# Selective scan in pieces of 447 nodes instead of 625, with the sum over the states moved from GpSimd to TensorE

## What is computed

```python
dA = jnp.exp(dt[:, :, None] * A)
dBx = (dt * xc)[:, :, None] * Bm[:, None, :]
def step(h, t):
    dA_t, dBx_t, C_t = t
    h = dA_t * h + dBx_t
    return (h, h @ C_t)
_, y = lax.scan(step, jnp.zeros((xc.shape[1], D_STATE), xs.dtype), (dA, dBx, Cm))
y = y + xc * D_param
y = y * jax.nn.silu(z)
```

## Time and profile before

| | us |
|---|---|
| median of 3 runs | 7942.77 (7941.25 to 7955.9) |
| profiled execution, its time | 7951.78 |
| its span, first to last instruction | 7950.2 |
| the scan, from its first spread matmul to its last `y` addition | 3454.0 to 4057.0 |
| the final multiplication by `z` ends | 4063.7 |

### The profile page before, as it was taken

The page is one execution under the profiler, slowest core; times in us unless marked ns, Lnnn a source line. Parts: engine busy times, 40 slices in busy tenths (PEclk is TensorE's granted clock), DMA queues, the critical chain, the costliest instruction groups (busy, mean ns, idle before and its releaser), DMA issues. The chain is left out here.

```text
span 7950.2 us, 67396 instructions
## 1 busy us (share of the span) xinstructions
PE 4464.4 (56%) x16661; PEld 3136.4 (39%) x16661; DVE 3856.6 (49%) x7877; ACT 2058.4 (26%) x4299; POOL 3287.4 (41%) x2886
## 2 busy tenths in 40 slices
PE   6699655438347750411117476985774864555263
PEld 3466433337235530200016343764553753333152
DVE  3244466411356556399953687226664025443212
ACT  4577200002123220321212111222331214444110
POOL 0666677331327740035530264005773024773313
PEclk8799777679767665655558698996675986666586
DMA  5233433446335541100030121004553534653254
GB/s 152 87 104 103 91 91 91 101 120 185 104 94 139 136 106 33 29 0 0 0 67 10 27 46 39 12 18 111 139 140 82 181 116 133 183 180 76 73 153 115
DMA packets 566098, 729.01 MB, mean 92 GB/s; under 512 B 197250, under 2 KB 424673, under 8 KB 562600
## 3 DMA queue, kind: packets, MB, share of 16 engines
q1 hardware_dynamic: 397770, 382.70, 17.2%
q0 software_dynamic: 168080, 343.54, 15.9%
HBM read 554.94 MB, written 174.38 MB: 92 GB/s over the span
## 5 line engine op out<-in xcount | busy, mean ns | idle before, releaser
L601 PE MATMUL ps<-msg,same 128*125 128x256 f32 (+2 forms) x3328 | 1354.2, 554 | 865.3 <-issue 325.4
L601 PEld LDWEIGHTS ps<-msg,same 128*125 128x125 f32 x3328 | 775.4, 261 | 1292.7 <-issue 697.5
L577 POOL DMA_INDIRECT msg<-d_gat,src_i x832 | 888.2, 1068 | 349.2 <-issue 232.8
L577 POOL DMA_INDIRECT msg<-d_lin,src_i x416 | 441.4, 1061 | 269.4 <-issue 120.8
L577 POOL DMA_INDIRECT msg<-rel_rows,src_rel x416 | 426.7, 1026 | 189.3 <-issue 116.1
L491 POOL DMA_INDIRECT rec<-rec,slot_i x391 | 412.8, 1056 | 193.0 <-issue 109.7
L1166 POOL DMA_DIRECT2D answered<-y x90 | 102.9, 1143 | 874.4 <-DVE y L1153 831.0
L1831 POOL TENSOR_TENSOR xc<-xc,dA 128x1250 f32<-128x1250 f32 x80 | 307.9, 3849 | 346.6 <-DVE dA L1899 346.6
L1844 PE MATMUL ps<-parts,sel 96*128 96x512 bf16 x320 | 97.9, 461 | 610.8 <-DVE dA L1899 489.1
L427 PE MATMUL ps_f<-w,hs 128*128 128x256 f32 x1568 | 393.1, 407 | 74.5 <-DVE hs L466 65.1
L1128 ACT ACTIVATE hid<-ps_h,b 128x250 f32<-128x250 f32 x380 | 178.2, 469 | 973.2 <-PE ps_h L1093 973.2
(11 more groups left out here) (551 smaller groups left out, 9096.6 us busy)
## 6 DMA issues: line engine op xcount, KB each, us to landing
lo_rows<-lo_r SPq DMA_DIRECT2D x208, 256.0 KB
fil<-rec SPq DMA_DIRECT2D x104, 512.0 KB
w<-in_L_ffn_w SPq DMA_DIRECT2D x80, 512.0 KB
w<-in_L_ffn_w SPq DMA_DIRECT2D x40, 1024.0 KB
rows<-sent SPq DMA_DIRECT2D x93, 250.0 KB
answered<-y POOLq DMA_DIRECT2D x90, 250.0 KB
rel_rows<-row SPq DMA_DIRECT2D x25, 896.0 KB
lo_rows<-ffn_lo_r SPq DMA_DIRECT2D x64, 250.0 KB
```

The costliest lines, as they stand in the source:

```text
L577: nc.gpsimd.indirect_dma_start(msg[:, g % R, j, :], None, table, bass.IndirectOffsetOnAxis(idx[:, n:n + 1], 0)).then_inc(msg_in[g % R], 16)
L601: nc.tensor.matmul(ps[:, j, 0:width], same[:, g % 2, j, :], msg[:, g % R, j, 0:width], start=True, stop=True).then_inc(mm, 1)
```

## The change

The loops are exchanged: the nodes are cut into seven pieces of 447 (the last has 443), and for each piece all 16 states are done, 112 steps in all. The step of VectorE writes its product into an own tile `pr`; TensorE multiplies it by the fp32 identity and accumulates it over the 16 states of a piece in `ps_y` (two fp32 matmuls of 447 columns). After a piece, `finish` adds `ps_y` to `y` and multiplies into `z`. ScalarE copies the last column of each state into `carry`, from which the next piece goes on. All 16 selectors are made ahead. B and C rows have PSUM buffers and semaphores of their own. The loops are written out instead of running as hardware loops; GpSimd has no work in the stage. The lines taken away are those of the function printed above; the diff is cut to what is added.

```diff
@@ selective_scan @@
-    SN, CH, NC = STATES, 625, 5
...
-                        nc.gpsimd.tensor_tensor(ycut, ycut, dA[:, b, :, :], ALU.add).then_inc(adds, 1)
...
+    nc = k.nc
+    SN, CH = STATES, 447
+    CUTS = [(lo, min(lo + CH, N)) for lo in range(0, N, CH)]
+    STEPS = len(CUTS) * SN
+    with stage(k) as s:
+        al, A = s.sb("al", [128, 2, SN]), s.sb("A", [128, 2, SN])
+        sel, mask = s.sb("sel", [DT_ROW, SN, 2, 128], BF16), s.sb("mask", [DT_ROW, BC])
+        dA, dB, hh, pr = (s.sb(n, [128, 2, 2, CH]) for n in ("dA", "dB", "hh", "pr"))
+        carry = s.sb("carry", [128, SN, 2])
+        ps_b, ps_c, ps_y = s.ps("ps_b", [128, 2, 512]), s.ps("ps_c", [128, 2, 512]), s.ps("ps_y", [128, 2, 512])
+        loaded, chain, raised, sels, exps, carried, ins_done, scanned, prods, b_mm, c_mm, y_mm, y_read = (
+            s.sem(n) for n in ("loaded", "chain", "raised", "sels", "exps", "carried", "ins", "scanned", "prods", "b_mm", "c_mm", "y_mm", "y_read"))
+        cut = lambda n: CUTS[n // SN]
+        size = lambda n: cut(n)[1] - cut(n)[0]
+        both = lambda row, m: row.unsqueeze(1).to_broadcast([128, 2, m])
             @block.sync
             def _(sp):
             @block.tensor
             def _(pe):
+                def spread_b(n):
+                    if n >= 2:
+                        pe.wait_ge(ins_done, n - 1)
+                    nc.tensor.matmul(ps_b[:, n % 2, 0:size(n)], sel[:, n % SN, 0, :], parts[:, cut(n)[0]:cut(n)[1]], start=True, stop=True).then_inc(b_mm, 1)
+                def spread_c(n):
+                    if n >= 2:
+                        pe.wait_ge(prods, n - 1)
+                    nc.tensor.matmul(ps_c[:, n % 2, 0:size(n)], sel[:, n % SN, 1, :], parts[:, cut(n)[0]:cut(n)[1]], start=True, stop=True).then_inc(c_mm, 1)
+                pe.wait_ge(sels, 1)
+                spread_b(0)
+                spread_b(1)
+                spread_c(0)
+                spread_c(1)
+                for n in range(STEPS):
+                    st, c = n % SN, n // SN
+                    if n + 2 < STEPS:
+                        spread_b(n + 2)
+                    pe.wait_ge(prods, n + 1)
+                    if n + 2 < STEPS:
+                        spread_c(n + 2)
+                    if st == 0 and c:
+                        pe.wait_ge(y_read, c)
+                    for h in range(2):
+                        ins = nc.tensor.matmul(ps_y[:, h, 0:size(n)], k.ident[:], pr[:, n % 2, h, 0:size(n)], start=st == 0, stop=st == SN - 1)
+                    ins.then_inc(y_mm, 1)
             @block.scalar
             def _(act):
+                def decays(n):
+                    if n >= 2:
+                        act.wait_ge(scanned, n - 1)
+                    for h in range(2):
+                        ins = nc.scalar.activation(dA[:, n % 2, h, 0:size(n)], dt[:, h, cut(n)[0]:cut(n)[1]], ACT.Exp, scale=A[:, h, n % SN:n % SN + 1])
+                    ins.then_inc(exps, 1)
+                nc.scalar.activation(A[:], al[:], ACT.Exp).then_inc(raised, 1)
+                act.wait_ge(sels, 1)
+                decays(0)
+                decays(1)
+                for n in range(STEPS):
+                    act.wait_ge(scanned, n + 1)
+                    nc.scalar.activation(carry[:, n % SN, :], hh[:, n % 2, :, size(n) - 1], ACT.Copy).then_inc(carried, 1)
+                    if n + 2 < STEPS:
+                        decays(n + 2)
             @block.vector
             def _(dve):
+                dve.wait_ge(raised, 1)
+                c_.step(nc.vector.tensor_scalar(A[:], A[:], -1.0, None, ALU.mult))
+                c_.link(nc.vector.tensor_tensor(mask[:], k.ident[0:DT_ROW, 0:BC], k.ident[0:DT_ROW, BC:2 * BC], ALU.add))
+                c_.link(nc.vector.tensor_tensor(mask[:], mask[:], k.ident[0:DT_ROW, 2 * BC:3 * BC], ALU.add))
+                for v in range(2):
+                    c_.step(nc.vector.tensor_copy(sel[:, :, v, :], mask[:, v * SN:(v + 1) * SN].unsqueeze(2).to_broadcast([DT_ROW, SN, 128])))
+                c_.wait()
+                dve.sem_inc(sels, 1)
+                def inputs(n):
+                    m = size(n)
+                    dve.wait_ge(b_mm, n + 1)
+                    if n >= 2:
+                        dve.wait_ge(scanned, n - 1)
+                    nc.vector.tensor_tensor(dB[:, n % 2, :, 0:m], both(ps_b[:, n % 2, 0:m], m), u[:, :, cut(n)[0]:cut(n)[1]], ALU.mult).then_inc(ins_done, 1)
+                def scan(n):
+                    st, m = n % SN, size(n)
+                    dve.wait_ge(exps, n + 1)
+                    dve.wait_ge(ins_done, n + 1)
+                    if n >= 2:
+                        dve.wait_ge(carried, n - 1)
+                        dve.wait_ge(prods, n - 1)
+                    for h in range(2):
+                        ins = nc.vector.tensor_tensor_scan(hh[:, n % 2, h, 0:m], dA[:, n % 2, h, 0:m], dB[:, n % 2, h, 0:m], carry[:, st, h:h + 1] if n >= SN else 0.0, ALU.mult, ALU.add)
+                    ins.then_inc(scanned, 1)
+                def product(n):
+                    m = size(n)
+                    dve.wait_ge(c_mm, n + 1)
+                    if n >= 2:
+                        dve.wait_ge(y_mm, n - 1)
+                    dve.wait_ge(scanned, n + 1)
+                    nc.vector.tensor_tensor(pr[:, n % 2, :, 0:m], both(ps_c[:, n % 2, 0:m], m), hh[:, n % 2, :, 0:m], ALU.mult).then_inc(prods, 1)
+                def finish(c):
+                    lo, hi = CUTS[c]
+                    dve.wait_ge(y_mm, SN * (c + 1))
+                    nc.vector.tensor_tensor(y[:, :, lo:hi], y[:, :, lo:hi], ps_y[:, :, 0:hi - lo], ALU.add).then_inc(y_read, 1)
+                    dve.wait_ge(y_read, c + 1)
+                    nc.vector.tensor_tensor(z[:, :, lo:hi], y[:, :, lo:hi], z[:, :, lo:hi], ALU.mult)
+                inputs(0)
+                inputs(1)
+                scan(0)
+                for n in range(STEPS):
+                    if n + 2 < STEPS:
+                        inputs(n + 2)
+                    if n + 1 < STEPS:
+                        scan(n + 1)
+                    if n % SN == 0 and n:
+                        finish(n // SN - 1)
+                    product(n)
+                finish(len(CUTS) - 1)
```

More of the change, by code:

```diff
@@ L1808, in selective_scan @@
     nc = k.nc
-    SN, CH, NC = STATES, 625, 5
-    CUT = [(0, 512), (512, CH - 512)]
+    SN, CH = STATES, 447
+    CUTS = [(lo, min(lo + CH, N)) for lo in range(0, N, CH)]
+    STEPS = len(CUTS) * SN
     with stage(k) as s:
[L1812 to L1817, removed]
+        al, A = s.sb("al", [128, 2, SN]), s.sb("A", [128, 2, SN])
[8 more added lines that the diff above has]
+        both = lambda row, m: row.unsqueeze(1).to_broadcast([128, 2, m])
         with s.block() as block:
@@ L1847, in _ @@
             @block.scalar
             def _(act):
-                act.wait_ge(loaded, 16)
[L1850 to L1858, removed]
+                def decays(n):
[4 more added lines that the diff above has]
+                    ins.then_inc(exps, 1)
```

## The result

| | before | after |
|---|---|---|
| median, us | 7942.01 (4 runs) | 8242.24 (4 runs) |
| profiled execution: time, span | 7951.78, 7950.2 | 8239.4, 8237.7 |
| scan stage, first spread matmul to end of the last multiplication by `z` | 3454.0 to 4063.7: 609.7 | 3448.15 to 4366.66: 918.5 |

The ratio is 1.038, with a 95% interval of 1.036 to 1.041. The forecast was 8256 us in a range of 8190 to 8310.

What follows compares the result with a forecast made beforehand. VectorE bounds the scan stage before; after, VectorE and TensorE take turns at 8.15 us a step, 109 such steps plus start, ends, finishes and casts making 923 us, 314 longer: 8256 us, range 8190 to 8310.

Steps and rivals of the forecast that it cites:

- The order of the queues: TensorE's B row of n + 3 stands behind y(n), so VectorE and TensorE take turns; VectorE idles 4.1 us a step.
- 109 waits of about 4 us: Sign in the scan stage: VectorE's inputs wait for TensorE's `ps_b` about 4 us, some 109 times, the stage's largest wait.
- The size of a step: Scan stage: inputs 0.98, scans 2.10, product to TensorE 1.13, TensorE to VectorE 3.94; sum 8.15 us a step.
- The clock: TensorE's clock in the scan stage stays near 0.50; rival: it rises, steps of 6.3 us, 8050 us, 11 in 100.
- GpSimd: Its additions hold up VectorE's scans in the kernel before, 135 of 578 busy us; without it scans have one speed.
- 5.54 us a step: VectorE's need in the kernel before without hold-ups: 1.35 + 1.35 + 2.84 us, 443 us for 80 steps.
- the 2.84 us: VectorE's two scans of 1250 elements in all, going on from a piece, kernel before; gives 2.10 us in the changed kernel.
- The rate of tensor_tensor: VectorE's inputs and product: 0.98 us each from the trace; by the skill's rule 1.09, sum about 25 us higher.
- The casts: Making the selectors: two casts of 2048 elements instead of 128, 0.21 + 2.0 us each, +4.0 us; lower bound 2.0.
- The stage's sum: Scan stage: 109 x 8.15 us plus start, ends, finishes and selectors, 923 us against 609.7 before, 314 us longer.
- The faster rival, with the B row in time: TensorE gives the B row before y(n): VectorE bounds at 4.06 us a step, stage 478 us, 7811 us; 6 in 100.
- ScalarE's copy: Two-number copy in the scan stage: with two Exp under 1.6 us a step, hidden, without table loads.

Runs made afterwards that it cites:

- small additions: Kernel before, with GpSimd's addition cut to 4 elements (2 columns of each half instead of 625): 7804.97 us in one run, against 7942.34.
- GpSimd at work beside the new order: Changed kernel with the B row issued ahead of the wait for product(n), plus one unused GpSimd addition a step: 7882.64 us, 0.995 of the kernel before.

## Why the prediction was right

*The order of the queues.* The B row of n + 3 behind y(n), behind product(n): shown from three sides, by moving the B row (stage 443 us shorter), by shortening what stands ahead of it (145 us) and by putting the scans beside it (272 us). The first rules out that TensorE's amount of work bounds the stage, the second that the wait is a fixed delay. The forecast of 109 waits of about 4 us stands against 110 waits and 436 us.

*The size of a step.* At the low clock it was 8.23 us for 8.15. The pieces: product's start to the start of TensorE's weight load 1.18 (forecast 1.13), TensorE to `inputs` 3.95 (3.94), inputs to scan 1.01 (0.98), scans 2.09 (2.10). The forecast had counted from TensorE's first matmul; so counted the first two are 1.21 and 3.92. Pieces cut to 447 cost VectorE what the element counts say, to 0.03 us an instruction. The mean over the stage (8.15) is lower for two reasons: the first piece's steps, whose scans start from a constant, take 8.11, and 24 steps, about every fifth, are 0.2 to 0.5 us shorter than their neighbours, where the clock rose in the last part of TensorE's run, as in the burst at 6943.56. Against these stand the finishes, six distances of 10.3 us, which the sum had counted apart, so the agreement of the mean with 8.15 is in part chance.

*The clock.* The forecast wanted it near 0.50, and the stage's mean is 0.60. That mean misleads, since most of the high stretches fell into TensorE's idle time. Weighted by the time of its matmuls the clock is 0.52. One of the short steps, TensorE's run and then the work of VectorE behind it:

```profile
3489.06:3492.47 3.41, 3.41 (x6) 1.45 (x6) 0.00 (x0) 0.23 (x1) 0.00 (x0) 0.59 0.00 0
3492.47:3496.70 4.23, 0.00 (x1) 0.03 (x1) 4.04 (x4) 1.09 (x3) 0.00 (x0) 0.83 0.00 0
```

So the forecast was right for TensorE's work: its runs began at the low clock, and only the ends of 24 of them, by 0.2 to 0.5 us, had the high one. The forecast had spoken of a clock near 0.50 without saying over which time.

*GpSimd.* That its additions made the slow scans is shown by the small additions (stage 153 us less, where the busy time had promised 135; the waits for ScalarE went too) and, from the other side, by GpSimd at work beside the new order. Two readings under it were off. Of the 135 us only 130 were GpSimd's doing (578 to 448): the other 5 are the small copies of `state`, which the prediction's 5.54 us a step left out. And the pair of scans of the earlier trace rows was not a quiet one. GpSimd's addition ran beside it:

```profile
3470.55 5.29 POOL L1831 TENSOR_TENSOR xc<-xc,dA 128x1250 f32<-128x1250 f32 x1 [4.11 <-DVE dA L1899]
```

There the scans kept their speed, and it was the addition that waited: 5.29 us, where the shortest took 2.40. So the 2.84 us are right for a pair that isn't held up, but the pair is no evidence from a time without GpSimd. Either engine can be the one that waits. In 47 of the 80 pairs the second scan was, at 3.6 or 4.0 us, and in 16 the first, at 2.7.

*The rate of tensor_tensor.* The Trainium skill's (N + 151)/0.96 ns (VectorE: DVE Perf Modes, the section on the TRN2 errata) gives 1.09 us for 894 elements. The trace agrees on the length (1.06 to 1.09), while the next instruction starts 1.01 us after it: the 25 us by which that rule would have raised the sum were not there.

*The casts.* The term that was mis-sized: two casts of 2048 elements, put at 2.2 us each, took 1.2 each, so the start cost 2 us where the sum had 4. The lower bound in the text had this.

```profile
3445.68 2.36 DVE L1882 CAST sel<-mask 96x2048 bf16<-96x2048 f32 x2
```

*The stage's sum.* From the first spread matmul 919 us were forecast (923 with the casts), 918.5 measured. That the two agree within 1 us is luck in part: steps dearer by 0.08 us cost about 8 us, and the 24 short ones gave 8 back. Of the 14 us between forecast and median, 2 are the casts and 1 the stage; the other 11 lie in the rest of the program, whose length varies more than that.

*The rivals.* The faster rival, with the B row in time, had been given a stage of 478 us and 7811; made into a kernel it measures 476.0 and 7811.39, and the second agreement is luck to the last digits, as its four runs lie between 7802 and 7823. The clock had been given 8050 and, forced, it measured 8056, but this near hit is luck too: the stage was 27 us longer than its price said, and a chip that runs the kernel before 16 us faster and a tail 14 us shorter than that of the kernel after made up for it. What decided against both was read in the code and in the trace: the place of one call in a queue, and the idle time between the bursts. ScalarE's copy took no table load in the stage and hid (0.21 us a step).

## What to carry over

When an engine that runs in order is given new work, look first at what stands behind it in its queue and who waits for that: here a matmul of 0.4 us that needed nothing stood behind 3 us of new work that depended on the waiting engine, and made two engines with 4 us of work each take turns. Issue what depends on nothing new ahead of the wait for the newest result; here its buffer had been free since inputs(n + 1). A sum of busy times (4.1 against 3.7 us a step) says nothing of this; walk through both queues for one step and write down who waits.

## What the hardware showed

GpSimd's addition and VectorE's scan, both with two operands in SBUF, don't run side by side: a 4-element addition waits out two scans (0.2 us becomes 2.76), and a scan waits for the end of an addition of 894 or 1250 elements (1.1 us becomes 2.2, and 1.5 becomes 4.0), while VectorE's multiplications with an operand in PSUM pass unhindered (1.07 us beside an addition). The Trainium skill (SBUF — State Buffer, section on the two separate sides) calls the pair of ports that the two engines share a lock held for a whole instruction; the trace agrees in that one of the two stood still until the other was done. When the turn changes isn't settled here: additions of 1250 elements mostly came between the two scans of a pair, those of 4 elements waited for both.

TensorE's clock was worth 178 us here, a factor of nearly two on the 3.7 us that stood in each step (8.23 us a step at the low clock, 6.39 at the high one), and matmuls whose result nobody reads bought it. With the C row moved away from ahead of the identity matmuls, their run took 0.16 us more (3.14 us for 2.98); that this is a weight load no longer covered is a reading, not shown by itself.
